# A fused attention and mixture-of-experts kernel: four reorderings in the order of work of three engines

## The reference

```
qk = silu(ln(x) @ Wqk.T + bqk);  v = silu(ln(x) @ Wv.T + bv)
quad_q, lin_q, quad_k, lin_k = rope(qk * gamma + beta)       # four of them
attn = relu(quad_q @ quad_k.T / 64 + bias) ** 2              # in groups of 64
u    = silu(ln(x) @ Wg.T + bg) * (attn @ v + lin_q @ (lin_k.T @ v / n))
x1   = layernorm(x + ln(u @ Wo.T + bo))
shared = gelu(x1 @ Wfc_s + bfc_s) @ Wproj_s + bproj_s        # hidden width 1024
gate   = the two largest of softmax(x1 @ Wr), of 8, made to sum to 1
routed = sum over experts e of gate[:, e] * (gelu(x1 @ Wfc[e] + bfc[e]) @ Wproj[e] + bproj[e])
out    = layernorm(x1 + shared + routed)
```

## Time and profile before

| | |
|---|---|
| median of 3 runs | 912.62 us (912.6 to 913.33) |
| profiled execution | 913.61 us, span 911.8 us |
| busy: TensorE, VectorE, ScalarE, GpSimd | 98%, 75%, 60%, 29% of the span |
| granted TensorE clock, mean | 0.996 of full |
| attention part | from 0 to 306.9 us |
| first shared block of the expert part | from 306.9 to 332.7 us |

### The profile page before, as it was taken

One profiled execution on the slowest core, in us unless ns is written; L12 is line 12 of the kernel. 1 busy time (PEld: TensorE's weight loads), 2 busy tenths in 40 slices (PEclk: granted clock), 3 DMA queues, 4 the chain that ended last, 5 costly groups with the idle time before them and its releaser, 6 DMA issues.

```text
span 911.8 us, 17334 instructions
## 1 busy us (share of the span) xinstructions
PE 891.1 (98%) x5792; PEld 795.0 (87%) x5792; DVE 684.0 (75%) x1684; ACT 550.2 (60%) x1015; POOL 268.4 (29%) x188
## 2 busy tenths in 40 slices
PE   8999999999999989999999999999999999999995
PEld 7778788888878879899999999999999999999985
DVE  7789889889888599676576675757655589997475
ACT  5646656756646746556556455555645568887475
POOL 0000011001010137347545254553534445542000
PEclk9999999999999999999999999999999999999999
DMA  5232233231225424539665464856577558776723
GB/s 169 87 133 70 76 107 107 75 124 66 96 93 195 162 49 86 130 106 259 151 209 132 155 206 98 248 144 189 135 236 190 135 140 233 227 214 198 238 70 116
DMA packets 70127, 133.36 MB, mean 146 GB/s; under 512 B 14334, under 2 KB 55095, under 8 KB 62776
## 3 DMA queue, kind: packets, MB, share of 16 engines
q1 hardware_dynamic: 49864, 107.68, 35.5%
q0 software_dynamic: 16512, 21.32, 14.0%
q10 hardware_dynamic: 3696, 3.67, 1.2%
HBM read 98.13 MB, written 33.46 MB: 144 GB/s over the span
## 4 chain that ended last, share of the span: by engine, by line
PE 57%; DVE 4%; DMA 2%; issue 1%; ACT 1%; DVEq 0%; ACTq 0%; SPq 0%
PE bank L1777 25%; PE bank L1852 25%; PE bank L1797 3%; PE bank L1803 3%; DMA k_wstage<-wall 2%; PE bank L1837 1%; DVE s_hl L1690 1%; PE bank L1875 0%; DVE s_y L1620 0%; DVE s_wfc0l L1587 0%; DVE s_y L1432 0%; DVE k_wfc1l L1587 0%; PE bank L1894 0%; ACT s_h L1372 0%; DVE s_wfc0h L1586 0%
## 5 line engine op out<-in xcount | busy, mean ns | idle before, releaser
L1372 ACT ACTIVATE s_h<-bank,k_bfc 128x512 f32<-128x512 f32 (+1 forms) x216 | 134.6, 623 | 199.4 <-PE bank L1852 194.1
L1690 DVE TENSOR_TENSOR s_hl<-s_h,s_hh 128x512 fp32r<-128x512 f32 (+1 forms) x204 | 123.5, 606 | 135.5 <-ACT s_hh L1376 134.3
L1236 POOL DMA_INDIRECT residual_sums<-s_y,s_dest x64 | 108.7, 1699 | 184.3 <-DVE s_y L1620 170.8
L1376 ACT ACTIVATE s_hh<-s_h 128x512 fp32r<-128x512 f32 (+1 forms) x216 | 122.9, 569 | 9.1
L1852 PE MATMUL bank<-k_uh,s_wfc0h 128*128 128x512 f32 (+1 forms) x384 | 120.3, 361 | 0.2 <-issue 0.2
L1777 PE MATMUL bank<-k_wpj1l,s_hh 128*128 128x256 f32 x384 | 109.3, 285 | 0.5 <-DVE s_hl L1690 0.4
L1777 PE MATMUL bank<-k_wpj1h,s_hh 128*128 128x256 f32 x384 | 108.5, 283 | 0.0
L1777 PE MATMUL bank<-k_wpj1h,s_hl 128*128 128x256 f32 x384 | 108.5, 283 | 0.0
L1777 PE MATMUL bank<-s_wpj0l,s_hh 128*128 128x256 f32 x344 | 96.6, 281 | 0.0
L1777 PE MATMUL bank<-s_wpj0h,s_hh 128*128 128x256 f32 x344 | 96.6, 281 | 0.0
L1777 PE MATMUL bank<-s_wpj0h,s_hl 128*128 128x256 f32 x344 | 96.5, 280 | 0.0
(11 more groups left out here) (357 smaller groups left out, 2245.6 us busy)
## 6 DMA issues: line engine op xcount, KB each, us to landing
k_wstage<-wall SPq DMA_DIRECT2D x42, 1024.0 KB, 6.3
s_acc<-wall SPq DMA_DIRECT2D x14, 1024.0 KB, 7.8
s_x_res<-x SPq DMA_DIRECT2D x8, 512.0 KB, 4.8
x_rows<-s_x SPq DMA_DIRECT2D x8, 512.0 KB, 3.3
residual_sums<-s_x SPq DMA_DIRECT2D x8, 512.0 KB, 4.2
x_parts<-s_x1h SPq DMA_DIRECT2D x8, 512.0 KB, 2.7
x_parts<-s_x1l SPq DMA_DIRECT2D x8, 512.0 KB, 3.7
k_uh<-x_parts SPq DMA_DIRECT2D x8, 512.0 KB, 5.3
```

The source lines that it names most:

```text
L1236: pool.indirect_dma_start(RES, bass.IndirectOffsetOnAxis(dest[:, at:at + 1].bitcast(U32), 0), y[:, t, :], None, bounds_check=N + S - 1, co ...
L1372: nc.scalar.activation(h[j % 2][:, cols], b[:, cols], ACT.Gelu_apprx_tanh, bias=bfc[w][:, j:j + 1]).then_inc(h_ev, 1)
L1376: nc.scalar.activation(hh[j % RING][:, cols], h[j % 2][:, cols], ACT.Copy).then_inc(hh_rd, 1)
L1690: tt(hl[j % RING][:, cols], h[j % 2][:, cols], hh[j % RING][:, cols].bitcast(F32), ALU.subtract).then_inc(hl_rd, 1)
```

## The change

1. On VectorE, in steps 1 to 7, `query_low` and the scores (now in `scores_squared`) come before the residual sums instead of behind them. Step 0 keeps its place.
2. On TensorE, `fc(0)` moves to the head of step 8, ahead of the logits transposes and the output product of that step; `fc(1)` stays where both were.
3. On TensorE, in steps 0 and 1 (main, but not `last`), the sixteen products of v and att for all four banks come first, and then, after the waits for `kvl` and the moved query, the four pairs of `kvh*lq` and `kvl*lq`. The other steps keep the old order.
4. In the expert part the running counts are issued behind chunk 6 of block 1 instead of behind chunk 5; on VectorE the copy of the triangle mask is cut out of `masks` and comes first, then `gates`, and the rest of `masks` last.

```diff
--- before.py
+++ after.py
@@ -615,6 +615,19 @@
                     dve.wait_ge(lqh_rd, b + 1)
                     tt(qkr[QK:P, 1, :], heads[QK:P, 0, :], lq[QK:P, :].bitcast(F32), ALU.subtract).then_inc(lql_rd, 1)
 
+                def scores_squared():
+                    dve.wait_ge(sc_mm, b + 1)
+                    sc = bank[5][:, :].rearrange("p (t n) -> p t n", t=TT)
+                    for g in range(P // G):
+                        r = slice(g * G, (g + 1) * G)
+                        last_i = stt(att[r, :, r], sc[r, :, r], 1.0 / G,
+                                     bias[r, :].rearrange("p (o n) -> p o n", o=1).to_broadcast([G, TT, G]), ALU.mult, ALU.add)
+                    link(last_i)
+                    for g in range(P // G):
+                        r = slice(g * G, (g + 1) * G)
+                        last_i = stt(att[r, :, r], att[r, :, r], 0.0, att[r, :, r], ALU.max, ALU.mult)
+                    last_i.then_inc(att_rd, 1)
+
                 if at(0):
                     query_low()
                     scales()
@@ -637,6 +650,9 @@
                         stt(z[:, t, :], yo[t], mean[:, TT + t:TT + t + 1], ln2[:, 0, :], ALU.subtract, ALU.mult).then_inc(o_ev, 1)
                     if at(B):
                         beside(2)
+                    if main:
+                        query_low()
+                        scores_squared()
                     dve.wait_ge(o_ev, 4 * b)
                     dve.wait_ge(res_rd, b)
                     for t in range(TT):
@@ -647,19 +663,8 @@
                 if main:
                     if at(0):
                         dve.wait_ge(ld_c, 16 * CONSTS)
-                    else:
-                        query_low()
-                    dve.wait_ge(sc_mm, b + 1)
-                    sc = bank[5][:, :].rearrange("p (t n) -> p t n", t=TT)
-                    for g in range(P // G):
-                        r = slice(g * G, (g + 1) * G)
-                        last_i = stt(att[r, :, r], sc[r, :, r], 1.0 / G,
-                                     bias[r, :].rearrange("p (o n) -> p o n", o=1).to_broadcast([G, TT, G]), ALU.mult, ALU.add)
-                    link(last_i)
-                    for g in range(P // G):
-                        r = slice(g * G, (g + 1) * G)
-                        last_i = stt(att[r, :, r], att[r, :, r], 0.0, att[r, :, r], ALU.max, ALU.mult)
-                    last_i.then_inc(att_rd, 1)
+                    if at(0):
+                        scores_squared()
                     dve.wait_ge(kv_ev, b + 1)
                     stt(kvl[:, :], bank[6][:, :], 1.0 / T, kvh[:, :].bitcast(F32), ALU.mult, ALU.subtract).then_inc(kvl_rd, 1)
                 if ahead:
@@ -782,6 +787,8 @@
                 main, ahead, o, last = stages(b)
                 c = b - 2
                 at = lambda n: is_int(b) and b == n
+                if at(B):
+                    fc(0)
                 if at(B + 2):
                     proj(KH - 1)
                 if main and at(0):
@@ -882,7 +889,7 @@
                 if main:
                     pe.wait_ge(att_rd, b + 1)
                 if at(B):
-                    beside(0, 1)
+                    fc(1)
                 if at(B + 1):
                     beside(6)
                 if last:
@@ -891,12 +898,25 @@
                         pe.wait_ge(x1T_ev, 2 * c)
                     transposes(x1, (4, 5), x1T_mm)
                 if main:
+                    if not last:
+                        for m in range(KE):
+                            if m < 3:
+                                pe.wait_ge(g_ev, 4 * b + m + 2)
+                            for t in range(TT):
+                                cols = slice(t * P, (t + 1) * P)
+                                mm(bank[1 + m][:, cols], v[:, t, m * P:(m + 1) * P], att[:, t, :], start=t == 0, stop=False,
+                                   skip_group_check=True)
                     pe.wait_ge(kvl_rd, b + 1)
                     pe.wait_ge(lq_rd, 16 * b + 16)
-                    for m in range(KE):
+                    if not last:
+                        for m in range(KE):
+                            rows = slice(m * P, (m + 1) * P)
+                            mm(bank[1 + m][:, :], kvh[:, rows], lq[:, :], start=False, stop=False, skip_group_check=True)
+                            mm(bank[1 + m][:, :], kvl[:, rows], lq[:, :], start=False, stop=True, skip_group_check=True).then_inc(u_mm, 1)
+                    for m in range(KE if last else 0):
                         if m < 3:
                             pe.wait_ge(g_ev, 4 * b + m + 2)
-                        elif last:
+                        else:
                             pe.wait_ge(x1T_ev, 2 * c + 1)
                         rows = slice(m * P, (m + 1) * P)
                         out = bank[1 + m]
@@ -1598,15 +1618,17 @@
                     link(tt(step_gate[:, 0:nt], step_gate[:, 0:nt], is_second, ALU.mult))
                     tt(gate[i][:, 0:nt], step_gate[:, 0:nt], first, ALU.add).then_inc(meta_rd, 1)
 
+            def triangle():
+                dve.wait_ge(ld_tri, 16)
+                nc.vector.tensor_copy(trib[:, :, :], tri[:, :, :]).then_inc(tri_rd, 1)
+
             def masks():
-                dve.wait_ge(ld_tri, 16)
                 dve.wait_ge(ld_ob, 32)
                 tt(gated_bias[0:NE, 0, :], gated_bias[0:NE, 0, :], gated_bias[0:NE, 1, :], ALU.add).then_inc(ob_rd, 1)
-                nc.vector.tensor_copy(trib[:, :, :], tri[:, :, :]).then_inc(tri_rd, 1)
                 nc.vector.tensor_copy(own_row[:, :], cst[:, TOK:TOK + NT]).then_inc(row_no_rd, 1)
 
 
-            beside = {(1, 0): lambda: choose(0), (1, 1): lambda: choose(1), (1, 2): lambda: (masks(), gates()),
+            beside = {(1, 0): lambda: choose(0), (1, 1): lambda: choose(1), (1, 2): lambda: (triangle(), gates(), masks()),
                       (1, 4): counts, (1, 5): starts, (1, 6): lambda: (small_starts(), slots_in_blocks()), (1, 7): slots, (2, 0): lambda: one_hots(0), **{(2, j + 4): lambda j=j: one_hots(j) for j in range(1, 4)},
                       (3, 0): lambda: one_hots(4), (3, 1): owners, **{(3, j - 3): lambda j=j: one_hots(j) for j in range(5, KH)},
                       (4, 0): slots_of_blocks}
@@ -1852,7 +1874,7 @@
                             last = mm(b[:, cols], wfc[w][ws][:, c, rows_], xs[i][:, c, cols], start=c == 0 and p == 0,
                                       stop=c == KD - 1 and p == 2)
                     last.then_inc(fc_mm, 1)
-                    if is_int(n) and n == 1 and j == 5:
+                    if is_int(n) and n == 1 and j == 6:
 
                         pe.wait_ge(both_rd, 1)
                         pe.wait_ge(tri_rd, 1)
```

## The result

The changed kernel takes 919.11 us (median of 7 runs, 917.04 to 920.06) where the kernel before, on the same chip, takes 913.33 us (7 runs, 911.92 to 916.18): a ratio of 1.0049, 95% interval 1.0035 to 1.0062. It is slower by about half a per cent. The profiled execution took 919.68 us with a span of 917.9, against 913.61 and 911.8 before: 6.1 us more in both.

The account below looks back on a forecast made before the run. TensorE, busy for 98% of the span, was taken as the bound, its stops summing to 7.1 us. Attention +5.6 less 2.1 in the expert part gave +3.5 us: 916.1 us, range 912.8 to 919.0.

Parts of the forecast that it names:

- the tail: Behind the stop at the ninth step's head: TensorE restarts at its lower clock level, costing 1.5 us more.
- The load in the way: Ninth step's head: fc(0) waits for the x1 parts until 275.9 instead of resuming at 272.02, 3.9 us later.
- The rival in which the data is there in time: Ninth step's head: x1 parts already in SBUF, the 1.1 us stop is won, 908.6 us in all; chance 8%.
- The rival of the longer slow stretch: Clock stays low for twice the 1.5 us, `hl` stops lower it too, only 1.4 won: 918.3 us; chance 13%.
- fc(0) in VectorE's chain: Ninth step: fc(0)'s 1.4 us stands ahead of VectorE's chain to the last x1; some 0.2 us shows.
- Products first, scores moved: First attention steps: TensorE gets 1.5 us ahead, of which 0.75 us is left from the third step on.
- The stop for `att`: Eighth step, before the transposes of x1: the 0.6 us stop becomes a wait for `kvl`, so nothing is won.
- the stop of 0.5 to 0.8 us for `kvl`: Sign of being right: a new TensorE stop of this size in the third and the eighth step.
- The moved scores alone: Squared scores ahead of the residual sums on VectorE: `att` comes 1.67 us earlier, gain costed at 0.
- Counts: First shared block of the expert part: stop for `both` falls from 3.85 to 0.5 us, TensorE 4.8 us ahead.
- The lead taken by VectorE: Expert part: fully booked VectorE stops TensorE at its `hl` halves; of 4.8 us lead, 2.1 us is gained.
- The gap of 2.09 us: Expert part: time from the end of VectorE's last half (360.17) to its projection (362.26), limiting the lead to 2.1 us.

Follow-up runs that it names:

- e1: Changed kernel with fc(0) back at its old place, the other three parts kept: 911.81 us against 914.24 for the kernel before, ratio 0.9975.
- e2: Kernel before with only fc(0) moved to the head of the ninth attention step: 920.25 us, ratio 1.0068 to the kernel before.
- e3: Changed kernel with the loads of batch 0's x1 parts issued one step earlier on SyncE: 910.8 us, ratio 0.9963 to the kernel before.
- e4: Changed kernel with 52 useless products in front of fc(0), filling the stop: 916.14 us, ratio 1.0014 to the kernel before.
- e10: Changed kernel with 26 useless products in front of fc(0), half filling the stop: 916.57 us, ratio 1.0028 to the kernel before.
- e8: Kernel before with only the attention products moved ahead of the kv products in the first two steps: one run, 912.82 us, span 911.0.
- e5: Kernel before with only the counts product one chunk on and the masks reordered: 911.38 us against 913.68, ratio 0.9989.
- e6: Kernel before with counts and masks changed, plus one-hot pieces one place later on VectorE and ScalarE's row numbers moved along: 909.63 us against 913.68, ratio 0.9964.

## Why the prediction was right, and where its sizes were off

The prediction said slower, 916.1 us in a range of 912.8 to 919.0. The direction and the cause held. The ratio of 1.0049 on the 912.62 us from which the prediction was made is 917.1 us, 1 us above the forecast; the medians differ by 5.8 us and the profiled executions by 6.1, where 3.5 was forecast. Against the profiled execution, which the sum was made for, 2.5 us are missing, and one term, the tail, is 1.4 of them; the rest is 0.5 at the load and 0.6 in the expert part.

- **The load in the way: right, slightly too small.** Forecast: resume at 275.9, +3.9. Measured: 276.44, +4.42. The store moved up by 0.57 (267.85 to 267.28) in place of 0.75, and the second load landed after 5.6 us in place of 5.3. 0.28 us of the 4.42 is only the later start of this trace, so the term itself was off by 0.2 to 0.3. e1 and e2 isolate it from both sides, and e3, which changes only when the loads are issued, removes the stop. The rival in which the data is there in time is excluded.
- **The tail: mechanism right, size wrong. This is the step that failed.** The prediction took 1.5 us from the stop of before for a stop 2.3 us longer. It was 2.9. The lowered level held until about 6 us behind the end of the stop here. e4 shows that standing idle causes it, since with the same data at nearly the same moment and TensorE busy the clock never falls. The rival of the longer slow stretch had named twice the 1.5, which is what came; the other half of that rival, stops for `hl` that lower the clock too, did not. The trace of before had a single stop of this kind; carrying its price over to a longer one was a guess, and the range had 3.0 as its end. What the price hangs on is the time that TensorE works at the lower level behind the stop (6.1 us here, 3.4 in e10), not a fixed amount per stop. The Trainium skill (TensorE: Matmul & The Clock Gate, Part 1) says that the array's clock is halved when TensorE has stood idle and comes back after sustained work; the traces agree, with windows at 0.50 and 0.68 behind the stop, and at 1.00 in e4.
- **fc(0) in VectorE's chain: 0.2, right.** From the resumption to the expert start the filled kernel took 35.05 us (276.03 to 311.08), the kernel before 34.88 (272.02 to 306.90). Attention in all: 4.42 + 2.9 + 0.2 = 7.5, where 5.6 was forecast.
- **Products first, scores moved: 0.75 forecast, 0.57 seen, 0.85 without the later start.** The stop for `att` turned into one for `kvl` of 0.54 us in the eighth step, as said. Missed: in the second step TensorE, being ahead, stopped 0.52 us for `s_z` at bank 6, a wait that the kernel before never had to make. It took that part of the lead one step before `kvl` would have, so the stop of 0.5 to 0.8 us for `kvl` that the prediction named for the third step as a sign did not come: the first u product starts 0.92 us behind the transposes of x1 (95.63 to 96.55), where before it was 0.79 (96.33 to 97.12). The lead that is left is close to the forecast all the same. The moved scores alone, costed at 0, were not tried; e8 shows that without them a stop of 0.35 us for `s_att` stands in the second step.
- **Counts: right.** 0.69 us of stop for a forecast 0.5, without a fall of the clock, and the cast behind GpSimd: 1.27 us at 329.35, while GpSimd works from 328.97 to 330.47. In the kernel before the same cast took 0.27 us at 323.09, with GpSimd done. The add, 1.36 us behind GpSimd before, now starts at 331.68, 0.1 us ahead of GpSimd's next operation, and takes 0.41. The Trainium skill (SBUF — State Buffer, Who interferes with whom) says the port pair is an exclusive lock for whoever starts first; the trace agrees, and moving an operation only changes which one is behind the lock: GpSimd's operation at 331.78 takes 1.46 us where the two after it take 1.3, and the cast of `own_row` behind it 1.25 us, where it took 0.16 before.
- **The lead taken by VectorE: right, 1.5 in place of 2.1.** The stops for `s_hl` came to 2.6 us. The gap of 2.09 us was read correctly, but VectorE's chain did not stay put: its half for project(3,0) starts 53.05 us behind the expert start (367.43), where before it started 52.59 behind (359.49). The trace shows how the 0.46 comes about. From its first `hl` half of the block (311.55 us before, 319.07 here) until this one VectorE never waits, so the shift is a sum of operations that became longer or shorter, mostly by about 1 us each, as they start while one of GpSimd's runs or no longer do. Counted from the expert start, `both` is made 0.32 us earlier than before; the copy of the counts, behind `own_row`, stands 1.2 us later; two small operations at 335.79 and 338.71, 1.22 and 1.14 us long in place of 0.17, make it 3.2; and others that had stood behind GpSimd before bring it back to 0.46 at the first half (357.88). e5 has the same 0.46. The prediction took this work as fixed in length; it was fixed only as long as it met GpSimd's at the same places. e6 shows that it is this chain that eats the lead: with the one-hots one place later 2.2 us more of the lead of 4.7 come through, 3.7 in all.

The sum as measured: +7.5 - 1.5 = +6.0 us against +5.6 - 2.1 = +3.5.

## What to carry to other kernels

Before work is moved to the head of an in-order engine, look up when its input lands and put it against the moment at which the engine gets there. A stop of some us costs its length and half of the time that TensorE then works at the lowered clock, and the price of one stop does not carry over to another (1.5 us behind 3.85, 1.7 behind 2.69, 2.9 behind 6.14). A stop that is covered shows the next one (`lgT` gave way to `s_z`, `both` to `s_hl`), so a lead is worth only what the tightest later meeting with another engine lets through: here the lead alone brought 1.5 us (e5), and moving the other engine's work brought 2.2 more (e6). And a stop that can't be avoided may be cheaper filled with useless products than left idle (e4: 3.0 us less).

## What the runs showed of the hardware

- Where a stop is shorter, the fall of the clock can come behind its end. In e10 the window of the 2.69 us stop reads 1.00 and the one after it 0.57; the first products behind the stop take 0.39 us and only later ones 0.63. In the changed kernel the window inside the stop already reads 0.54.
- Two stops of nearly the same length at the same place cost 2.0 us (5.78, e2) and 2.9 us (6.14). In e2 the windows of 272 to 276 and of 280 to 284 us read 0.76 and 0.89, in the changed kernel 0.54 and 0.68: the clock fell later in e2 and rose sooner. What sets these moments stays open.
- An operation of VectorE that falls behind one of GpSimd's can take about 1 us more, however small it is: the cast of 128x32 elements took 0.16 us before, with GpSimd idle, and 1.25 after, started 0.24 us into an operation of GpSimd's.
